# Loads and stores on one ring: all transfers issued by SyncE in a fixed order

## The reference

```python
def reference(x):
    return x + wavelet_pyramid(group_norm(x, G=16, eps=1e-5))

def wavelet_pyramid(v):            # three levels
    result = v
    for level in range(3):
        sh, sw = H // 2**level, W // 2**level
        approx = conv3x3(result[:, :, :sh, :sw], outer([.25, .5, .25]))   # zero padded
        result[:, :, :sh//2, :sw//2] = approx[:, :, ::2, ::2]
    return result
```

## Time and profile before

| what | value |
|---|---|
| median of 3 runs | 1297.73 us (1297.19 to 1298.64) |
| the profiled execution's own time | 1298.64 us |
| its span, first to last instruction | 1296.6 us |
| PE / DVE / ACT / POOL busy | 95% / 85% / 88% / 37% |
| DMA: moved | 537.03 MB, mean 414 GB/s |
| mean busy share of the 16 DMA engines, queue q1 and queue q10 | 50.7% and 50.4% |
| granted TensorE clock | 0.989 |

### The profile page before, as it was taken

One profiled execution on the slowest core, in us unless ns is written; L12 is line 12 of the kernel. 1 busy time (PEld: TensorE's weight loads), 2 busy tenths in 40 slices (PEclk: granted clock), 3 DMA queues, 4 the chain that ended last, 5 costly groups with the idle time before them and its releaser, 6 DMA issues.

```text
span 1296.6 us, 19103 instructions
## 1 busy us (share of the span) xinstructions
PE 1236.5 (95%) x5632; PEld 705.0 (54%) x5632; DVE 1102.9 (85%) x1536; ACT 1140.2 (88%) x1282; POOL 479.2 (37%) x1316
## 2 busy tenths in 40 slices
PE   5999999999999999999999999999999999999996
PEld 2555555555555555555555555555555555555553
DVE  5888889888888888888888888888888887888874
ACT  4999999999999999999988989889898988989985
POOL 3433433433433334334343443434333343334431
PEclk9999999999999999999999999999999999999998
DMA  9999999999999999999999999999999999999996
GB/s 373 408 415 419 420 421 421 421 421 421 421 422 421 421 421 421 421 421 421 421 421 421 421 421 421 422 421 421 419 421 420 415 419 418 414 421 414 419 397 268
DMA packets 135212, 537.03 MB, mean 414 GB/s; under 512 B 4128, under 2 KB 4128, under 8 KB 135200
## 3 DMA queue, kind: packets, MB, share of 16 engines
q1 hardware_dynamic: 67584, 268.44, 50.7%
q10 hardware_dynamic: 67616, 268.44, 50.4%
HBM read 268.44 MB, written 268.44 MB: 414 GB/s over the span
## 4 chain that ended last, share of the span: by engine, by line
PE 41%; ACT 25%; DMA 20%; issue 9%; ACTq 2%; DVE 2%; DVEq 0%
DMA y_dram<-xs 14%; ACT xs L478 13%; PE l_ps L362 7%; PE l_ps L370 7%; DMA xs<-x_dram 7%; PE l_ps L361 6%; PE l_ps L365 6%; PE l_ps L367 6%; ACT l L451 5%; PE l_ps L398 3%; ACT squares L439 3%; ACT l L466 3%; PE var_ps L377 2%; PE l_ps L399 2%; PE l_ps L400 2%
## 5 line engine op out<-in xcount | busy, mean ns | idle before, releaser
L439 ACT ACTIVATE squares<-xs,negm 128x4096 bf16<-128x4096 f32 x128 | 474.8, 3709 | 4.2
L249 POOL TENSOR_TENSOR l<-l,col_fix 128x4 f32<-128x4 f32 x128 | 158.7, 1240 | 760.9 <-ACT l L451 760.9
L305 DVE SCALAR_TENSOR_TENSOR h<-xs 128x2048 f32<-128x2048 f32 x128 | 294.7, 2302 | 29.7 <-DMA xs<-x_dram 26.3
L311 DVE SCALAR_TENSOR_TENSOR h<-xs,h 128x2040 f32<-128x2040 f32 x128 | 291.0, 2274 | 0.0
L478 ACT ACTIVATE xs<-xs,negmr,r_plus 128x2048 f32<-128x2048 f32 x128 | 267.8, 2092 | 0.0
L292 DVE SCALAR_TENSOR_TENSOR xs<-l_ps,r,xs 64x256 f32<-64x256 f32 x256 | 123.0, 480 | 124.0 <-PE l_ps L401 122.1
L473 ACT ACTIVATE xs<-xs,negmr,r_plus 128x1024 f32<-128x1024 f32 x128 | 157.6, 1231 | 46.2 <-issue 46.1
L317 DVE SCALAR_TENSOR_TENSOR a<-h 128x1024 f32<-128x1024 f32 x128 | 157.6, 1231 | 4.4
L450 ACT ACTIVATE l<-l_ps,negm_e 128x512 f32<-128x512 f32 x128 | 87.6, 685 | 72.1 <-PE l_ps L370 72.0
L217 POOL TENSOR_TENSOR newt<-r,half_t 128x1 f32<-128x1 f32 x128 | 147.5, 1152 | 0.0
L362 PE MATMUL l_ps<-h,w_even 128*64 128x512 f32 x256 | 141.1, 633 | 0.0
(11 more groups left out here) (83 smaller groups left out, 2161.3 us busy)
## 6 DMA issues: line engine op xcount, KB each, us to landing
xs<-x_dram SPq DMA_DIRECT2D x128, 2048.0 KB, 15.1
y_dram<-xs ACTq DMA_DIRECT2D x126, 2048.0 KB, 34.7
y_dram<-xs ACTq DMA_DIRECT2D x4, 1024.0 KB, 8.7
```

Of the source, the lines that this page charges most:

```text
L249: nc.gpsimd.tensor_tensor(col, col, col_fix[:, b], ALU.add).then_inc(l1_fixed, 1)
L305: nc.vector.scalar_tensor_tensor(h1[:, b], v[:, :, 0:W:2], 2.0, v[:, :, 1:W:2], ALU.mult, ALU.add).then_inc(h1_part, 1)
L311: nc.vector.scalar_tensor_tensor(h1[:, b, :, 1:W1], v[:, :, 1:W - 2:2], 1.0, h1[:, b, :, 1:W1], ALU.mult, ALU.add, accum_out=hsum[:, b:b + ...
L439: nc.scalar.activation(squares[:], xs[:, u % SLOTS, :], ACT.Square, bias=negm[:, b:b + 1], accum_out=sumsq[:, b:b + 1]).then_inc(sumsq_rea ...
```

## The change

All transfers are issued by SP, so they stand in one ring, and ACT issues none. SP first issues the loads of groups 0 to 7. Then for each group k in order it issues the store of k, as soon as the three semaphores allow it, and behind it, from k = 1 on, the load of group k+7, as soon as the store of group k-1, which used that slot, has landed. After the load of group 127 there are only stores left: those of groups 121 to 125 and the four halves of the last two groups. The waits of a store are the same as before, but SP holds them now. Nothing is changed on PE, DVE and POOL.

```diff
--- before.py
+++ after.py
@@ -138,15 +138,40 @@
 
         @block.sync
         def _(sp):
-            def load(lap, slot):
-                if later(lap, 0, 1):
+            def load(n):
+                lap, slot = divmod(n, SLOTS)
+                if lap:
                     sp.wait_ge(x_stored[slot], 16 * lap)
                 sp.dma_start(whole(slot), x_dram[lap, slot]).then_inc(x_loaded[slot], 16)
 
-            for lap in range(LAPS):
-                for slot in range(SLOTS):
-                    load(lap, slot)
-
+            def store(n):
+                lap, slot = divmod(n, SLOTS)
+                sp.wait_ge(scaled, n + 1)
+                sp.wait_ge(l1_added, n + 1)
+                sp.wait_ge(l2_added, n + 1)
+                sp.dma_start(out_dram[lap, slot], whole(slot)).then_inc(x_stored[slot], 16)
+
+
+            def store_half(n, f):
+                lap, slot = divmod(n, SLOTS)
+                sp.wait_ge(scaled, n + 1)
+                if f == 0:
+                    sp.wait_ge(l1_added, n + 1)
+                    sp.wait_ge(l2_added, n + 1)
+                sp.dma_start(out_half[lap, slot, f], half_of(slot, f)).then_inc(x_stored[slot], 16)
+
+            for n in range(SLOTS):
+                load(n)
+
+            for n in range(G - LAG_L3):
+                store(n)
+                if 1 <= n < G - SLOTS + 1:
+                    load(n + SLOTS - 1)
+
+            store_half(G - 2, 1)
+            store_half(G - 1, 1)
+            store_half(G - 2, 0)
+            store_half(G - 1, 0)
 
             for slot in range(SLOTS):
                 sp.wait_ge(x_stored[slot], 16 * (LAPS + (slot >= SLOTS - LAG_L3)))
@@ -478,31 +503,11 @@
                 nc.scalar.activation(bottom, bottom, ACT.Identity, bias=negmr[:, c],
                                      scale=r_plus1[:, c]).then_inc(scaled, 1)
 
-            def store(lap, k):
-                n = lap * SLOTS + k
-                slot, back = k % SLOTS, k // SLOTS
-                act.wait_ge(scaled, n + 1)
-                act.wait_ge(l1_added, n + 1)
-                act.wait_ge(l2_added, n + 1)
-                nc.scalar.dma_start(out_dram[lap + back, slot], whole(slot)).then_inc(x_stored[slot], 16)
-
-
-            def store_half(lap, k, f):
-                n = lap * SLOTS + k
-                slot, back = k % SLOTS, k // SLOTS
-                act.wait_ge(scaled, n + 1)
-                if f == 0:
-                    act.wait_ge(l1_added, n + 1)
-                    act.wait_ge(l2_added, n + 1)
-                nc.scalar.dma_start(out_half[lap + back, slot, f], half_of(slot, f)).then_inc(x_stored[slot], 16)
-
             def step(lap, u):
                 base = lap * SLOTS
                 make, done = exists(base, u), exists(base, u - LAG)
                 if make:
                     moments(base, u)
-                if exists(base, u - LAG_L3):
-                    store(lap, u - LAG_L3)
                 if done:
                     scale_beside(base, u - LAG)
                 if make:
@@ -517,13 +522,9 @@
             with act.Fori(1, LAPS) as lap:
                 for u in range(SLOTS):
                     step(lap, u)
-            store_half(LAPS, -2, 1)
             scale_beside(G, -1)
             scale_bottom(G, -1)
-            store_half(LAPS, -1, 1)
             evacuate2(G, -1)
-            store_half(LAPS, -2, 0)
-            store_half(LAPS, -1, 0)
 
 
 def kernel(x):
```

## The result

The changed kernel takes 1300.75 us (median of 22 runs) against 1297.77 us of the kernel before. The ratio is 1.004 with an interval of 1.0027 to 1.0054: slower by 0.4%, where 0.6% faster was forecast. The profiled execution took 1303.61 us with a span of 1301.9, so the two traces differ by 5.0 us where the medians differ by 3.0.

What follows compares the result with a forecast made beforehand. It took the DMA transfers as the bound, one engine having fallen behind, at 10.09 us per pair. 46.5 + 124 x 10.03 = 1290.2, stated as 1290.5 us; range 1281 to 1312, the forecast's own 1285 to 1295.

Steps and rivals of the forecast that it cites:

- p: Time of one load and store pair in the new order: 10.03 us at 418 GB/s, against 10.09 before.
- the gain is that all sixteen engines share it: In the mixed stretch, all DMA engines would share the work, for a price of 0.07 us per pair.
- the 1.5 us left over: Remainder of the 1296.6 us span after eight loads and 124 pairs, kept as the end.
- The tail: After the last load, seven groups of stores, 35 us, would fill the end on all engines.
- The 13.9 us to be won: Gain at the end: 35 us of stores less 21.1 us for 8.90 MB at 421 GB/s.
- The slow DMA engine stays slow: Rival, chance 0.20: one engine needs 10.09 us per pair in any order, the others wait; time stays 1297.7 us.
- One ring is not slower than two: Denies a rival, chance 0.30: one ring moves 411 GB/s, 10.20 us per pair, 1311.3 us.
- ACT's issues off its stream: ACT loses 130 issues of 0.38 to 1.76 us; costed at nothing, steps of 9.68 us being already shorter.
- the steps stayed covered: About 65 us lie between a group's load and its store's turn; the first group needed 36.89 us.
- the ring did not run dry: When a store lands, two transfers or 10 us of work still stand in the ring.
- Stores land after 19.6 us and not 10 to 15: Sign in the later profile: stores would land some 10 to 15 us after their issue, not 35.
- stores were late for their turn: Early stores were 2.3 and 2.7 us early; lateness from slow starts taken as zero, 2 us as upper end.

Runs made afterwards that it cites:

- bf16_after: The changed kernel with the tiles that PE reads and the weights in bfloat16; 1308.02 us, ratio to the kernel before 1.0052 to 1.0097.
- dma_all: dma_one_ring with PE, ACT, DVE and POOL computing beside it on their own tiles, without waits between them and the transfers; 1299.88 us.
- dma_tiny: dma_one_ring with ACT and DVE running about 22,000 operations of one element per partition beside it; 1315.63 us.
- after_reversed: The changed kernel with the groups taken from the other end of the arrays, group 127's addresses first; 1309.47 us.
- bf16_before: The kernel before with the tiles that PE reads and the weights in bfloat16, weights made by POOL; 1296.05 us.
- bf16_act: bf16_before with its eleven bfloat16 weights made by ACT in place of POOL; 1291.62 us.
- order_two_rings: The kernel before, ACT still issuing stores, but the load of group k+7 also waits until the store of k is ready; 1300.72 us.
- dma_one_ring: The changed kernel without its computation, a store waiting only for its own load; 1284.61 us, ratio to the kernel before 0.9887 to 0.9920.

## Why the prediction was wrong

**The step that failed** is p, in the sentence "the gain is that all sixteen engines share it". The engines do not share: each carries its sixteenth of every transfer, and the lagging one cannot hand any of it on. Its own pace, 10.09 us per pair before, set the end in both orders. p came out at 10.08 on the mean instead of 10.03, which is 6.2 of the 10.25 us by which the forecast missed. That the profile held two numbers that do not agree, 421 GB/s and a spacing of 10.09, was seen; read to its end, it says that the fifteen store faster than the loads come. The eighth engine had landed store 20 at 245.5 us and store 80 at 834.0, 9.81 per group; 2.097 MB in 9.81 us and 2.097 MB in 10.09 us are 421 GB/s. The difference goes into a lead, and only the sixteenth engine counts. Two readings hid it. The slices of the earlier trace rows fall not only in the last two but from the thirty-second on (414 to 421 before those two), where the lead no longer grows as it did: 13.2 us at store 60, 19.5 at 80, 24.2 at 100, 22.1 at 120. And 10.09 is the pace of ten loads; over all loads it is 10.06, so the end behind the last load was larger than the 1.5 us left over, by 0.03 x 124, about 4 us.

**The tail** was mis-sized with it. The 13.9 us to be won were idle time of the fifteen. The last load landed 33.2 us ahead of the end before (1263.4 of 1296.6) and 35.7 us after (1266.2 of 1301.9): in both the lagging engine stored seven groups one after the other.

**The rival that held** is "The slow DMA engine stays slow": 416 GB/s with loads every 10.09 us was its sign, and 500 to 1000 us show 416 with 10.09 on the mean. Its time, 1297.7, missed by 3.0 us. The evidence against it, that nothing shows the engine behind in the first stretch, was no evidence: a lag that grows by a quarter of a microsecond per group is not seen there.

**The 3 us on top** no rival had. In the changed kernel the last ten loads took 10.37 us each, 0.28 more than the pace of the earlier trace rows; over ten groups that is 2.8 us. It is the second loss of the experiments: bf16_after, dma_all, dma_tiny and after_reversed have such stretches of 10.3 to 10.5 us, and the kernel before, bf16_before and bf16_act, with two rings and no tie, do not. order_two_rings, with the tie and two rings, loses the same 3 us, but has no such stretch (10.12 us from 800 us on, where the kernel before has 10.06). So it is shown that both kernels with the fixed order lose some 3 us, and not how. That it takes away a lead with which the fifteen ran through disturbances does not hold for order_two_rings, which kept its lead. What slows the late stretch stays open.

**One ring is not slower than two.** This rival had 0.30 and fell: a pair takes 9.94 us in one ring, 9.95 in two. The 411 GB/s of eight loads alone belonged to loads without stores. Here the rule of the Trainium skill (DMA: Bandwidth & Descriptors, "Issuing engines are not separate DMA queues") was the better guide, and these two runs agree with it in their pace.

**What was right:** ACT's issues off its stream gained nothing that the traces show; the steps stayed covered; the ring did not run dry; and the fifteen engines were held within one transfer of the slowest, 4 us in place of 24. Two sizes were off. Stores land after 19.6 us and not 10 to 15, since four transfers stand in the ring when one is issued, the store itself included. And stores were late for their turn 24 times in the first 300 us, in slices at 408 to 420 GB/s where the kernel before had 408 to 421; by these slices it cost about 1 us.

## What to carry to other kernels

A rate over all DMA engines can look full while one engine decides: multiply the spacing of the transfers by the rate, and where that is more than the bytes of one round, look for the engine that works alone at the end (a stretch at one sixteenth of the rate). An order that ties loads closely to stores does not speed that engine up; it only makes the others wait for it. Where transfers bound the kernel and engines run beside them, fewer and longer instructions can be worth having even on an engine that has time to spare: bf16_act gained 0.5%, though the same tiles in the fixed order gained nothing.

## What the runs showed of the hardware

In these runs one DMA engine falls behind beside executed instructions. Set against dma_one_ring by the time of the last load (1232.6 us), 22,860 more instructions of one element cost 29.5 us (dma_tiny, last load at 1262.1), of which 8.7 us fell when none was executed any more, so at most 0.9 ns each; 4,637 with POOL's tiny operations 2.7 us, 0.6 ns; 5,023 with wide products 1.8 us, 0.4 ns; 2,579 with long operations of ACT and DVE nothing. SP's fulfilled waits cost by far the most, 31.2 us for 4,096 recorded instructions (last load at 1279.5 against 1248.3), the fetching of their code included. So the count explains the direction, but the price depends on the kind. A late stretch of 10.3 to 10.5 us per load, in dma_tiny with no instruction beside it, is a loss that instructions executed at the time do not explain. Whether an instruction itself or the record that the profiler keeps of it reaches the DMA engine is not separated: each execution here has its span and granted clock from such records, and none was timed without. That, which engine it is, and why the loss of the fixed order varies so much (1299.15 to 1311.88 us in runs of the changed kernel, 1296.69 to 1298.75 in runs of the kernel before), stays open.
